# An expert gate that multiplies the centred values and applies 1/std afterwards, in a two-block image kernel on one core

## The chip, the core and the metric

The kernel runs on one core of a Trainium2 chip, as one program. The metric is the device time in microseconds (us) of one execution; lower is better. Seven instruction streams matter here: PE (TensorE, matrix products) with PEld (its weight loads), DVE (VectorE), ACT (ScalarE), POOL (GpSimd), SP (the queue that issues most transfers), and the 16 DMA engines behind them. Every tensor is float32. Each float32 matrix product shows as two records in the trace; a transpose shows as one.

## The reference, cut to what matters

x has 8 images, 32 channels and 24x24 = 576 pixels. Four blocks follow one another, each on normalized values and each added to x: a 3x3 neighbourhood attention, a mixture of 16 experts, a convolution-like block, and a chain of up to 33 data-dependent steps. The change is in the second, which computes, for a layer norm over the 32 channels of each pixel (token):

```
t = (v - mean) / sqrt(var + 1e-5)                 # per token
logits = t @ gate_w.T + gate_b                    # (image, token, expert)
probs  = softmax(logits, over the 576 tokens)
topv, topi = top 8 tokens of each (image, expert)
pooled = sum over the 8 tokens of topv * t[topi]  # (image, expert, channel)
out    = MLP of the expert (weight1, gelu, weight2) on pooled
result[topi] += out * topv
```

The value 1/std belongs to one token of one image; it is the same for all 32 channels and for all 16 experts. The gate bias belongs to one expert, and is the same for all tokens.

## The kernel before, in words

**Layout.** The 8 images are cut into T = 2 halves of TB = 4 images; a half lies as 128 partitions (4 images x 32 channels) by 576 pixels, so a value tile is [128, 2, 576]. The gate's results lie the other way: 128 rows, one per (expert, image) pair, by 576 tokens (`logit`, `rest`, `pick`). A bank of the accumulation memory PS holds 512 values, so a row of 576 takes two products of HS = 288 columns, g = 0 and 1, in two banks.

**Layer norm i** (i = 1 is the one before the experts) goes through three engines. PE centres the values by a product with the matrix `cen` (L621 for i = 0, 2, 3; for i = 1 the products are L729, one for each partial sum of the attention's taps, so that the centred sum grows in PS while the taps come in). ACT squares them from PS (L1067) and copies them to `xc` (L1070). PE sums the squares over channels (`variances`, L631, into 32 rows for each quarter of the pixels, 144 columns). ACT takes the root (L1076), DVE the reciprocal `rstd` (L1238), PE widens it back to 128 rows (`widen`, L644), and DVE multiplies: y = xc * 1/std (L1259). The function `keep_clock` (L615) issues products whose result nobody reads.

**Order.** Each engine runs a list written out by hand, and waits on semaphores. There is no planner. For the expert block PE's list is: the last taps (L729), `variances(1)`, `widen(1)`, the gate product of y (L793, two halves, two products each), ten transposes of y (L800), `preload(0)` (L786, copies centred values into the banks into which results are later added), two products of `keep_clock`, the five transposing products of `pick` with `share` (L811: the selected weights turned to tokens by rows, and divided by the softmax's sum), one `keep_clock`, ten pooling products (L821), and then the expert MLP (L835 to L851) and the scatter (L827). ACT's list is: squares, copy, squares, root, copy of the second half (L1070), load of the table for Exp (L1081), the two halves of `logit` with the bias (L1117), Exp with its sum (L1120), `share` (L1123), three copies of the transposed y to `yT` (L1127), load of the table for Gelu. DVE's list is: `rstd`, y (two halves), the eight largest logits (L1317), their first negated (L1319), the mark of the eight (L1320), the reciprocal of the sum (L1323), `pick` = the eight probabilities, two halves (L1326), the copy of the transposed picks (L1330). POOL meanwhile adds up x after the attention (L559, L563), which ACT waits for at L1129 to L1130. The constants come in three transfers, of which the last, from `hsum` to the table's end (L434), is first needed by the attention's score sums (L711).

Of the kernel before, what the change touches and what calls it, by code (L numbers as in the profile page):

```python
# [7 lines left out]
B, C, HH, WW = 8, 32, 24, 24  # L8
S = HH * WW
P = 128  # L10
# [28 lines left out]
_COLS = [("idn", P), ("cen", P), ("mean", T * 32), ("heads", T * P), ("hsum", T * 32), ("own", B), ("blk", GV), ("blk_end", GV_END),  # L39
         ("ebias", P), ("istep", NB_)]  # L40
OFF, _o = {}, 0
# [6 lines left out]
def constant_table():  # L48
# [32 lines left out]
    e = np.arange(E_)  # L81
    put("ebias", (e[:, None] == p[None, :] // B).astype(np.float32))
    put("istep", 4 * NOPS * np.arange(NB_, dtype=np.float32)[None, :])
    return t
# [7 lines left out]
def metaformer(nc, x, L0_conv_W_trans, L0_ffn_gate_w, L0_ffn_gate_b, L0_ffn_weight1, L0_ffn_weight2,  # L92
# [7 lines left out]
    with ctx:  # L100
# [40 lines left out]
        share = sb("share", [P, P])  # L141
        prob = sb("prob", [P, S])
        pick = sb("pick", [P, S])
# [107 lines left out]
        wc_rep = sem("wc_rep")  # L251
        tail_rdy, bc_ld, bc_set = (sem(n) for n in ("tail_rdy", "bc_ld", "bc_set"))
        row2_done, row2_rdy, row3_rdy = (sem(n) for n in ("row2_done", "row2_rdy", "row3_rdy"))
        waited, wide_first = sem("waited"), sem("wide_first")
# [31 lines left out]

        XB, VB = ((0, 2), (2, 0), (0, 6), (0, 2)), (4, 4, 2, 4)

        def cut(a, t):
# [49 lines left out]
        MAB_BANK = [6, 7, 5, 0, 1]  # L339
        PICK_BANK = (7, 2)  # L340
        PROB_BANK = 2
# [268 lines left out]
        def _(pe):  # L610
# [13 lines left out]
            def variances(i):  # L624

                mean = con("mean").rearrange("p (t m) -> p t m", t=T)
                for t in range(T):
                    for q in range(4):
                        if q % 2 == 0:
                            pe.wait_ge(sq_rdy, 2 * (T * i + t) + q // 2 + 1)  # L630
                        last = nc.tensor.matmul(PS[32 * q:32 * q + 32, VB[i], 0:QS], mean[:, t, :], sq[:, t, q * QS:(q + 1) * QS],  # L631
                                                start=(t == 0), stop=(t == T - 1), skip_group_check=True)
                last.then_inc(var_rdy, 1)
                if i != 2:
                    keep_clock(2, VB[i] + 1)
                    keep_clock(1, VB[i] + 1, 96)

            def widen(i):
# [9 lines left out]
                last.then_inc(rwide_rdy, 1)  # L648
                if i < 2:
                    pe.wait_ge(xc_copied, T * i + 1)  # L650
                    keep_clock(1, XB[i][0] + 1)
# [126 lines left out]
            pe.wait_ge(vadd_rdy, 1)  # L778
            add_tap(14, last=True)
            variances(1)  # L780
            widen(1)


# [4 lines left out]

            for t in range(T):
                pe.wait_ge(xc_copied, 2 * T)  # L790
                pe.wait_ge(y_rdy, T + t + 1)
                for g in range(2):
                    last = nc.tensor.matmul(PS[:, g, 0:HS], gate_bd[:, t, :], cut(y, t)[:, g, :],  # L793
                                            start=(t == 0), stop=(t == T - 1), skip_group_check=True)
                    if t == T - 1:
                        last.then_inc(logit_done, 1)
            for c in range(FULL + 1):
                w = P if c < FULL else TAIL
                for t in range(T):
                    last = nc.tensor.transpose(PS[0:w, 4 + c // 2, ((c % 2) * T + t) * P:((c % 2) * T + t + 1) * P],  # L800
                                               y[:, t, c * P:c * P + w], idn)
                if c % 2 or c == FULL:
                    last.then_inc(yT_done, 1)
            pe.wait_ge(logit_rdy, 2)
            preload(0)
            keep_clock(2, 7)
            pe.wait_ge(share_rdy, 1)
            for c in range(FULL + 1):
                w = P if c < FULL else TAIL
                pe.wait_ge(pick_rdy, 1 if c * P + w <= HS else 2)  # L810
                last = nc.tensor.matmul(PS[0:w, PICK_BANK[c // FULL], (c % FULL) * P:(c % FULL + 1) * P], pick[:, c * P:c * P + w],  # L811
                                        share[:, :], start=True, stop=True, skip_group_check=True)
                if c >= FULL - 1:
                    last.then_inc(pickT_done, 1)
# [51 lines left out]
            def pixels_out(i):  # L866

                if i < T:
                    pe.wait_ge(scat_copied, i + 1)
                pe.wait_ge(y_rdy, 2 * T + T * (i + 1 if i < 2 else NP))  # L870
                for t in range(T):
# [187 lines left out]
        def _(act):  # L1059
            act.dma_start(cst[:, 0:OFF["mean"][0]], consts[:, 0:OFF["mean"][0]]).then_inc(c0_in, 16)  # L1060
            act.dma_start(x_in[:, 1, :], x[TB:B].rearrange("b c h w -> (b c) (h w)")).then_inc(x_ld[2], 16)
            def layernorm(i, eps):
# [13 lines left out]
                nc.scalar.activation(std[:, :], PS[:, VB[i], 0:QS], ACT.Sqrt, bias=eps[:, :]).then_inc(std_rdy, 1)  # L1076
                keep(1)

# [34 lines left out]
            load_table(ACT.Exp)  # L1113
            act.wait_ge(gb_ld, 16)
            for g in range(2):
                act.wait_ge(logit_done, g + 1)
                nc.scalar.activation(logit[:, g * HS:(g + 1) * HS], PS[:, g, 0:HS], ACT.Identity,  # L1117
                                     bias=gb[:, :]).then_inc(logit_rdy, 1)
            act.wait_ge(ntop_rdy, 1)
            nc.scalar.activation(half(0, PROB_BANK), flat2(logit[:, :]), ACT.Exp, bias=ntop[:, :],  # L1120
                                 accum_out=psum_[:, :]).then_inc(prob_rdy, 1)
            act.wait_ge(prec_rdy, 1)
            nc.scalar.activation(share[:, :], idn, ACT.Copy, scale=prec[:, :]).then_inc(share_rdy, 1)  # L1123
            for c in range(0, FULL + 1, 2):
                act.wait_ge(yT_done, c // 2 + 1)
                n, w = (2, P) if c < FULL else (1, TAIL)
                nc.scalar.copy(yT[0:w, c:c + n, :, :].rearrange("k c t p -> k (c t p)"), PS[0:w, 4 + c // 2, 0:n * T * P]).then_inc(yT_rdy, 1)  # L1127
            load_table(ACT.Gelu)
# [99 lines left out]
        def _(dve):  # L1228
# [7 lines left out]
            def layernorm(i, dst, between=None):  # L1236
# [8 lines left out]
                if between:  # L1245
                    between()
                dve.wait_ge(rwide_rdy, i + 1)
                if i == 2:
                    dve.wait_ge(xc_copied, T * i + T)
# [64 lines left out]

            layernorm(1, y)
            dve.wait_ge(logit_rdy, 2)
            nc.vector.max(top8[:, :], logit[:, :]).then_inc(top_rdy, 1)  # L1317
            dve.wait_ge(top_rdy, 1)
            nc.vector.tensor_scalar(ntop[:, :], top8[:, 0:1], -1.0, None, ALU.mult).then_inc(ntop_rdy, 1)  # L1319
            nc.vector.match_replace(rest[:, :], top8[:, :], logit[:, :], -3e38).then_inc(rest_rdy, 1)  # L1320
# [220 lines left out]
```

## Time and profile before

| | |
|---|---|
| median of 3 runs | 117.33 us (117.3 to 118.57) |
| the profiled execution | 117.42 us |
| its span in the trace | 115.4 us |
| PE, DVE, ACT, POOL busy in the span | 102.5, 64.9, 48.3, 65.3 us |
| granted clock of PE | full in all 40 slices |
| expert block, from the last taps' end to the scatter's first product | 50.09 to 69.74 us |

The span is what the trace covers; some 2.0 us of the profiled execution lie around it. "Busy" is the union of an engine's instructions. A busy PE is not a PE at its peak, since the ends of pipelined products are modelled and products that only keep the engine running count too. Times in the trace count from the span's start.

### The profile page before, as it was taken

What the parts mean: (1) busy time and instruction counts of PE and PEld (TensorE: products, weight loads), DVE (VectorE), ACT (ScalarE), POOL (GpSimd) and SP (SyncE); (2) the same over time, 40 slices, a digit from 0 to 9 for tenths busy, and PEclk for the clock granted to TensorE, in tenths of its full rate; (3) what the DMA queues carried; (4) which work ended last, traced back from release to release, by engine and by line L of the source; (5) the groups of instructions that cost most, each with busy time, mean ns of one, the idle gap of its engine ahead of it and who ended that gap; (6) DMA issues with size and microseconds to landing.
All of it is one profiled execution on the core that took longest, in us unless ns stands there. A gap on an engine that the chain in (4) does not pass through costs nothing.

```text
span 115.4 us, 2257 instructions
## 1 busy us (share of the span) xinstructions
PE 102.5 (89%) x825; PEld 66.9 (58%) x825; DVE 64.9 (56%) x150; ACT 48.3 (42%) x103; POOL 65.3 (57%) x68
## 2 busy tenths in 40 slices
PE   6999897986889899998999999898999989986870
PEld 4666654756525347665877675453489766563350
DVE  0019389979589999116263402379716555145891
ACT  4268260209300004055379465622430263685743
POOL 8992079800457988999992000099999950007300
PEclk9999999999999999999999999999999999999999
DMA  3934600000000000000000000000000000100005
GB/s 92 304 27 79 119 0 6 0 6 0 0 0 0 3 0 0 6 0 0 0 0 3 0 6 0 0 3 0 0 6 0 0 0 0 29 6 3 0 6 204
DMA packets 7148, 2.61 MB, mean 23 GB/s; under 512 B 5454, under 2 KB 6624, under 8 KB 7137
## 3 DMA queue, kind: packets, MB, share of 16 engines
q1 hardware_dynamic: 6849, 2.04, 7.7%
q10 hardware_dynamic: 288, 0.43, 1.0%
q8 instruction: 7, 0.11, 0.4%
q14 instruction: 4, 0.03, 0.1%
HBM read 1.87 MB, written 0.59 MB: 21 GB/s over the span
## 4 chain that ended last, share of the span: by engine, by line
PE 58%; DVE 26%; ACT 6%; issue 5%; POOL 2%; DVEq 1%; ACTq 0%; POOLq 0%
DVE prods L1269 7%; PE PS L901 6%; PE PS L744 5%; PE PS L729 5%; PE PS L621 5%; PE PS L615 5%; DVE prods L1307 4%; DVE rstd L1238 4%; PE PS L882 3%; PE PS L827 3%; PE PS L631 3%; PE PS L821 2%; PE PS L644 2%; PE PS L722 2%; PE PS L874 2%
## 5 line engine op out<-in xcount | busy, mean ns | idle before, releaser
L1067 ACT ACTIVATE sq<-PS 128x288 f32<-128x288 f32 x16 | 6.4, 416 | 24.3 <-PE PS L729 18.4
L615 PE MATMUL PS<-sq 128*128 128x288 f32 (+1 forms) x44 | 14.6, 452 | 1.1 <-POOL sq L494 1.1
L1307 DVE TENSOR_TENSOR prods<-PS,vpad 128x432 f32<-128x432 f32 x24 | 12.8, 600 | 1.9 <-PE PS L744 1.6
L535 POOL TENSOR_TENSOR prods<-prods 128x576 f32<-128x576 f32 x8 | 11.7, 1479 | 3.0 <-DVE prods L1307 2.9
L729 PE MATMUL PS<-prods,cst 128*128 128x288 f32 x44 | 12.4, 420 | 0.2 <-POOL prods L535 0.2
L574 POOL TENSOR_TENSOR x<-h,x 128x192 f32<-128x192 f32 x6 | 4.5, 776 | 13.7 <-ACT h L1149 13.6
L729 PEld LDWEIGHTS PS<-prods,cst 128*128 128x128 f32 x44 | 7.8, 189 | 5.5 <-POOL prods L535 1.9
L521 POOL TENSOR_TENSOR prods<-q_sb,kpad 128x576 f32<-128x576 f32 x6 | 7.7, 1320 | 5.6 <-ACT kpad L1095 5.6
L615 PEld LDWEIGHTS PS<-sq 128*128 128x128 f32 x44 | 8.2, 208 | 4.1 <-POOL sq L494 1.1
L1238 DVE RECIPROCAL rstd<-std 128x144 f32<-128x144 f32 x4 | 4.2, 1053 | 11.4 <-ACT std L1076 11.3
L563 POOL TENSOR_TENSOR x<-x,prods 128x576 f32<-128x576 f32 x7 | 9.8, 1405 | 0.5
L1081 ACT ACT_TABLE_LOAD x7 | 9.0, 1283 | 2.2 <-PEq L1524 1.7
L414 POOL TENSOR_TENSOR y<-x,h 128x192 f32<-128x192 f32 x6 | 3.3, 593 | 10.7 <-DVE h L1259 10.7
L1269 DVE TENSOR_TENSOR prods<-PS,kpad 128x576 f32<-128x576 f32 x12 | 8.1, 749 | 2.3 <-ACT kpad L1095 2.3
L744 PE MATMUL PS<-attn,cst 32*128 32x432 f32 x48 | 7.0, 571 | 1.1 <-DVE prods L1307 0.5
L901 PE MATMUL PS<-prods,xT 128*126 128x190 f32 (+3 forms) x46 | 7.4, 310 | 0.0
L528 POOL TENSOR_TENSOR attn<-att,srec 128x432 f32<-128x432 f32 x2 | 2.6, 1302 | 7.7 <-DVE srec L1294 7.7
L685 PE MATMUL PS<-y,qkv_bd 128*128 128x288 f32 x24 | 6.6, 419 | 0.3 <-DVE y L1259 0.3
L1369 DVE TENSOR_TENSOR gram<-PS,cst 126x760 f32<-126x760 f32 (+1 forms) x5 | 4.4, 870 | 4.3 <-PE PS L901 4.3
L711 PE MATMUL PS<-prods,cst 128*32 128x144 f32 x144 | 5.9, 291 | 0.9 <-DVE prods L1269 0.8
L901 PEld LDWEIGHTS PS<-prods,xT 128*126 128x126 f32 (+1 forms) x46 | 6.3, 185 | 0.6 <-issue 0.6
L1172 ACT COPY prods<-PS 64x252 f32<-64x252 f32 (+1 forms) x10 | 3.5, 346 | 7.7 <-PE PS L912 7.6
(166 smaller groups left out, 195.1 us busy)
## 6 DMA issues: line engine op xcount, KB each, us to landing
result<-y SPq DMA_DIRECT2D x2, 288.0 KB, 2.1
prods<-in_x SPq DMA_DIRECT2D x2, 144.0 KB, 2.9
prods<-in_x ACTq DMA_DIRECT2D x1, 288.0 KB, 3.6
cst<-consts SPq DMA_DIRECT2D x1, 261.5 KB, 2.9
ew<-in_L_ffn_weight SPq DMA_DIRECT2D x4, 64.0 KB, 2.3
ew<-in_L_ffn_weight SPq DMA_DIRECT2D x1, 256.0 KB, 2.9
cst<-consts SPq DMA_DIRECT2D x1, 160.0 KB, 2.4
cst<-consts ACTq DMA_DIRECT2D x1, 128.0 KB, 2.9
```

The lines of the kernel that those rows point to most:

```text
L521: nc.gpsimd.tensor_tensor(prods[:, t, n, :].rearrange("p (r c) -> p r c", c=WW), q_sb[:, t, :].rearrange("p (r c) -> p r c", c=WW), kpad[: ...
L535: return nc.gpsimd.tensor_tensor(tap(a), tap(a), tap(b), ALU.add).then_inc(padd_rdy, 1)
L563: last = nc.gpsimd.tensor_tensor(total, total, tap(n), ALU.add)
L615: nc.tensor.matmul(PS[:, bank, 0:width], sq[:, 0, 0:P], sq[:, 0, 0:width], start=True, stop=True)
L685: last = nc.tensor.matmul(PS[:, bank + g, 0:HS], qkv_bd[:, w, :], cut(y, t)[:, g, :], start=True, stop=True)
L729: done = nc.tensor.matmul(PS[:, XB[1][t] + g, 0:HS], con("cen"), src[:, g * HS:(g + 1) * HS], start=first, stop=last, skip_group_check=True)
L744: last = nc.tensor.matmul(PS[:, ring(2 * g + h)[q % 2], 0:TRI * QS], band_of(t, q), attn[32 * q:32 * q + 32, m * TRI:(m + 1) * TRI, :], st ...
L901: last = nc.tensor.matmul(PS[0:w, GRAM_BANK[k] + i // 2, (i % 2) * GV + lo:(i % 2) * GV + hi], xT[:, cols], uT[:, (g0 + i) * GV + lo:(g0 + ...
L1081: nc.scalar.activation(tab[:, :], tab[:, :], f)
L1238: nc.vector.reciprocal(rstd[:, :], std[:, :]).then_inc(rstd_rdy, 1)
L1269: nc.vector.tensor_tensor(prods[:, t, n, :].rearrange("p (g r c) -> p g r c", g=2, c=WW), rows24(half(t, Q_BANK, 4)), kpad[:, t, dy:dy + H ...
L1307: nc.vector.tensor_tensor(prods[:, t, m * TRI:(m + 1) * TRI, q * QS:(q + 1) * QS].rearrange("p n (r c) -> p n r c", c=WW), PS[:, ring(2 * ...
```

## The change

The gate product now reads the centred values `xc` instead of y, and 1/std is applied to its result, in the rows of (expert, image) pairs. A new constant `rows_e` (128 more columns, at the end part of the table) spreads `rstd` to those rows; four products do it in place of eight. DVE's two products that made y are gone; two products of 288 columns make `logit` from the copied gate result and the spread 1/std in PS. `pick` is kept for the scatter, and a scaled `pick_n` = pick * 1/std goes into the pooling, which now reads the transposed `xc`. The bias no longer goes into `logit`; two instructions on 128x1 keep the shift of Exp. The second half of `xc` is copied by DVE in two pieces instead of by ACT. The transposes go to banks 0 and 1, and ACT's copies of them stand ahead of Exp instead of behind `share`. `gate(0)` stands ahead of `variances(1)` in PE's list and `gate(1)` behind it; the three `keep_clock` products of `variances(1)` and the one of `widen(1)` are gone.

```diff
@@ tiles, constant and helpers
-_COLS = [..., ("ebias", P), ("istep", NB_)]
+_COLS = [..., ("ebias", P), ("rows_e", P), ("istep", NB_)]
+    img = (p % 32) // HEADS
+    put("rows_e", ((p[:, None] % HEADS == 0) & (img[:, None] == p[None, :] % B)).astype(np.float32))
+        def by_expert(q):
+            return cst[32 * q:32 * q + 32, OFF["rows_e"][0]:OFF["rows_e"][1]]
+        def wide_e(g):
+            return PS[:, VB[1] + 2 * g:VB[1] + 2 * g + 2, 0:QS]
+        def two(a):
+            return a.rearrange("p (u s) -> p u s", u=2)
-        PICK_BANK = (7, 2)
+        PICK_BANK = (4, 2)
+        GATE_BANK = 2
+        TURN_BANK = (0, 1, 0)
@@ PE: variances, widen
-                if i != 2:
+                if i in (0, 3):
                     keep_clock(2, VB[i] + 1)
                     keep_clock(1, VB[i] + 1, 96)
...
-                if i < 2:
+                if i == 0:
                     pe.wait_ge(xc_copied, T * i + 1)
                     keep_clock(1, XB[i][0] + 1)
@@ PE: the expert block
             add_tap(14, last=True)
+            def gate(t):
+                pe.wait_ge(xc_copied, T + t + 1)
+                for g in range(2):
+                    last = nc.tensor.matmul(PS[:, GATE_BANK + g, 0:HS], gate_bd[:, t, :], cut(xc, t)[:, g, :],
+                                            start=(t == 0), stop=(t == T - 1), skip_group_check=True)
+                    if t == T - 1:
+                        last.then_inc(logit_done, 1)
+            gate(0)
             variances(1)
-            widen(1)
+            gate(1)
+            pe.wait_ge(rstd_rdy, 2)
+            for q in range(4):
+                last = nc.tensor.matmul(PS[:, VB[1] + q, 0:QS], by_expert(q), rstd[32 * q:32 * q + 32, :],
+                                        start=True, stop=True, skip_group_check=True)
+            last.then_inc(rwide_rdy, 1)
-            for t in range(T):
-                pe.wait_ge(xc_copied, 2 * T)
-                pe.wait_ge(y_rdy, T + t + 1)
-                for g in range(2):
-                    last = nc.tensor.matmul(PS[:, g, 0:HS], gate_bd[:, t, :], cut(y, t)[:, g, :],
...
             for c in range(FULL + 1):
                 w = P if c < FULL else TAIL
+                if c == FULL:
+                    pe.wait_ge(yT_rdy, 1)
                 for t in range(T):
-                    last = nc.tensor.transpose(PS[0:w, 4 + c // 2, ...], y[:, t, c * P:c * P + w], idn)
+                    last = nc.tensor.transpose(PS[0:w, TURN_BANK[c // 2], ...], xc[:, t, c * P:c * P + w], idn)
...
-            pe.wait_ge(logit_rdy, 2)
+            pe.wait_ge(yT_rdy, 3)
+            keep_clock(2, 1)
             preload(0)
-            keep_clock(2, 7)
             pe.wait_ge(share_rdy, 1)
             for c in range(FULL + 1):
                 w = P if c < FULL else TAIL
-                pe.wait_ge(pick_rdy, 1 if c * P + w <= HS else 2)
-                last = nc.tensor.matmul(..., pick[:, c * P:c * P + w],
+                pe.wait_ge(pickn_rdy, 1 if c * P + w <= HS else 2)
+                last = nc.tensor.matmul(..., pick_n[:, c * P:c * P + w],
                                         share[:, :], start=True, stop=True, skip_group_check=True)
@@ ACT
-                keep(1)
+                if i != 1:
+                    keep(1)
...
             load_table(ACT.Exp)
-            act.wait_ge(gb_ld, 16)
             for g in range(2):
                 act.wait_ge(logit_done, g + 1)
-                nc.scalar.activation(logit[:, g * HS:(g + 1) * HS], PS[:, g, 0:HS], ACT.Identity, bias=gb[:, :]).then_inc(logit_rdy, 1)
+                nc.scalar.copy(gated[:, g * HS:(g + 1) * HS], PS[:, GATE_BANK + g, 0:HS]).then_inc(gate_copied, 1)
+            for c in range(0, FULL + 1, 2):
+                act.wait_ge(yT_done, c // 2 + 1)
+                ... # the three copies to yT, which stood behind share before
             act.wait_ge(ntop_rdy, 1)
-            nc.scalar.activation(half(0, PROB_BANK), flat2(logit[:, :]), ACT.Exp, bias=ntop[:, :],
+            nc.scalar.activation(half(0, PROB_BANK), flat2(logit[:, :]), ACT.Exp, bias=shift[:, :],
                                  accum_out=psum_[:, :]).then_inc(prob_rdy, 1)
@@ DVE: layernorm, expert block
                 dve.wait_ge(rwide_rdy, i + 1)
+                if i == 1:
+                    for g in range(2):
+                        dve.wait_ge(gate_copied, g + 1)
+                        nc.vector.tensor_tensor(two(logit[:, g * HS:(g + 1) * HS]), two(gated[:, g * HS:(g + 1) * HS]), wide_e(g),
+                                                ALU.mult).then_inc(logit_rdy, 1)
+                    return
...
-            layernorm(1, y)
+            for g in range(2):
+                dve.wait_ge(sq_rdy, 2 * (T + 1) + g + 1)
+                last = nc.vector.tensor_copy(cut(xc, 1)[:, g, :], PS[:, XB[1][1] + g, 0:HS])
+            last.then_inc(xc_copied, 1)
+            layernorm(1, None)
             dve.wait_ge(logit_rdy, 2)
             nc.vector.max(top8[:, :], logit[:, :]).then_inc(top_rdy, 1)
             dve.wait_ge(top_rdy, 1)
-            nc.vector.tensor_scalar(ntop[:, :], top8[:, 0:1], -1.0, None, ALU.mult).then_inc(ntop_rdy, 1)
+            dve.wait_ge(gb_ld, 16)
+            nc.vector.tensor_scalar(ntop[:, :], top8[:, 0:1], gb[:, :], -1.0, ALU.add, ALU.mult).then_inc(max_rdy, 1)
+            dve.wait_ge(max_rdy, 1)
+            nc.vector.tensor_tensor(shift[:, :], ntop[:, :], gb[:, :], ALU.add).then_inc(ntop_rdy, 1)
             nc.vector.match_replace(rest[:, :], top8[:, :], logit[:, :], -3e38).then_inc(rest_rdy, 1)
...
                                                ALU.is_le, ALU.mult).then_inc(pick_rdy, 1)
+                dve.wait_ge(pick_rdy, g + 1)
+                nc.vector.tensor_tensor(two(pick_n[:, cells]), two(pick[:, cells]), wide_e(g), ALU.mult).then_inc(pickn_rdy, 1)
```

## Rows read from the trace of the kernel before

**Rows 1.** Part 1 of the page: busy time of each engine

```profile
PE 102.5 (89%) x825; PEld 66.9 (58%) x825; DVE 64.9 (56%) x150; ACT 48.3 (42%) x103; POOL 65.3 (57%) x68
```

**Rows 2.** Chain of waits, last taps to gate: start us, length us, engine, line, count

```profile
47.88 2.21 PE PS L729 x8
50.09 0.96 PE PS L631 x16
51.08 0.39 ACT std L1076
51.49 1.06 DVE rstd L1238
52.60 0.82 PE PS L644 x16
53.44 0.77 DVE y L1259
54.34 1.71 PE PS L793 x6
```

**Rows 3.** Chain of waits, logits to pooling and on

```profile
56.14 0.94 ACT logit L1117 x2
57.09 0.77 DVE top L1317
57.89 0.17 DVE ntop L1319
58.08 0.88 ACT PS L1120 x2
59.72 1.51 PE PS L811 x10
61.91 2.88 PE PS L821 x20
```

**Rows 4.** Timeline, PE: start us, us, op, shapes, count [idle before]

```profile
7.88 0.77 PE L631 MATMUL PS<-sq,cst 128*32 128x144 f32 x16
```

**Rows 5.** Timeline, ACT and PE: table loads, copies, transposes

```profile
49.64 0.90 ACT L1067 ACTIVATE sq<-PS 128x288 f32<-128x288 f32 x2 [3.89 <-PE PS L729]
51.36 0.63 ACT L1070 COPY xc<-PS 128x576 f32<-128x576 f32 x1
60.88 1.28 ACT L1081 ACT_TABLE_LOAD   x1
62.29 1.14 ACT L1132 COPY prods<-wcT 128x1152 f32<-128x1152 f32 x1
71.76 0.73 ACT L1067 ACTIVATE sq<-PS 128x288 f32<-128x288 f32 x2
56.36 1.25 PE L800 MATMUL PS<-cst,y 128*128 128x128 f32 x10
59.55 1.31 ACT L1127 COPY yT<-PS 128x512 f32<-128x512 f32 x3
```

**Rows 6.** Chain of waits, the last layer norm's widening, four products

```profile
102.48 0.57 PE PS L644 x8
```

**Rows 7.** Groups by form, 44 to 77 us: mean ns of one after the busy time

```profile
L1326 DVE SCALAR_TENSOR_TENSOR pick<-rest,PS 128x288 f32<-128x288 f32 x2 | 0.8, 442 | 0.0
L1330 DVE COPY pickT<-PS 128x512 f32<-128x512 f32 x1 | 0.7, 692 | 1.0 <-PE PS L811 1.0
```

**Rows 8.** Timeline, DVE and POOL: last sum of taps; sum of x; picks

```profile
45.81 0.76 DVE L1312 TENSOR_TENSOR prods<-prods 128x576 f32<-128x576 f32 x1
56.66 4.38 POOL L563 TENSOR_TENSOR x<-x,prods 128x576 f32<-128x576 f32 x3
59.13 0.80 DVE L1326 SCALAR_TENSOR_TENSOR pick<-rest,PS 128x288 f32<-128x288 f32 x2
```

**Rows 9.** PE's waits by line: us in total, times, longest us

```profile
PE PS L722 <- ACT att L1106: 1.5, 1, 1.5
...
PE PS L711 <- DVE prods L1269: 0.8, 4, 0.2
```

More of the change, by code:

```diff
@@ L39 @@
 _COLS = [("idn", P), ("cen", P), ("mean", T * 32), ("heads", T * P), ("hsum", T * 32), ("own", B), ("blk", GV), ("blk_end", GV_END),
-         ("ebias", P), ("istep", NB_)]
+         ("ebias", P), ("rows_e", P), ("istep", NB_)]
 OFF, _o = {}, 0
@@ L141, in metaformer @@
         share = sb("share", [P, P])
-        prob = sb("prob", [P, S])
+        pick_n = sb("pick_n", [P, S])
+        shift = sb("shift", [P, 1])
+        gated = sb("gated", [P, S])
         pick = sb("pick", [P, S])
@@ L252, in metaformer @@
         tail_rdy, bc_ld, bc_set = (sem(n) for n in ("tail_rdy", "bc_ld", "bc_set"))
+        gate_copied, max_rdy, pickn_rdy = (sem(n) for n in ("gate_copied", "max_rdy", "pickn_rdy"))
         row2_done, row2_rdy, row3_rdy = (sem(n) for n in ("row2_done", "row2_rdy", "row3_rdy"))
@@ L787, in preload @@
                                      skip_group_check=True)
-            for t in range(T):
-                pe.wait_ge(xc_copied, 2 * T)
-                pe.wait_ge(y_rdy, T + t + 1)
-                for g in range(2):
-                    last = nc.tensor.matmul(PS[:, g, 0:HS], gate_bd[:, t, :], cut(y, t)[:, g, :],
-                                            start=(t == 0), stop=(t == T - 1), skip_group_check=True)
-                    if t == T - 1:
-                        last.then_inc(logit_done, 1)
             for c in range(FULL + 1):
                 w = P if c < FULL else TAIL
+                if c == FULL:
+                    pe.wait_ge(yT_rdy, 1)
                 for t in range(T):
-                    last = nc.tensor.transpose(PS[0:w, 4 + c // 2, ((c % 2) * T + t) * P:((c % 2) * T + t + 1) * P],
-                                               y[:, t, c * P:c * P + w], idn)
+                    last = nc.tensor.transpose(PS[0:w, TURN_BANK[c // 2], ((c % 2) * T + t) * P:((c % 2) * T + t + 1) * P],
+                                               xc[:, t, c * P:c * P + w], idn)
                 if c % 2 or c == FULL:
                     last.then_inc(yT_done, 1)
-            pe.wait_ge(logit_rdy, 2)
+            pe.wait_ge(yT_rdy, 3)
+            keep_clock(2, 1)
             preload(0)
-            keep_clock(2, 7)
             pe.wait_ge(share_rdy, 1)
@@ L809, in _ @@
                 w = P if c < FULL else TAIL
-                pe.wait_ge(pick_rdy, 1 if c * P + w <= HS else 2)
-                last = nc.tensor.matmul(PS[0:w, PICK_BANK[c // FULL], (c % FULL) * P:(c % FULL + 1) * P], pick[:, c * P:c * P + w],
+                pe.wait_ge(pickn_rdy, 1 if c * P + w <= HS else 2)
+                last = nc.tensor.matmul(PS[0:w, PICK_BANK[c // FULL], (c % FULL) * P:(c % FULL + 1) * P], pick_n[:, c * P:c * P + w],
                                         share[:, :], start=True, stop=True, skip_group_check=True)
@@ L869, in pixels_out @@
                     pe.wait_ge(scat_copied, i + 1)
-                pe.wait_ge(y_rdy, 2 * T + T * (i + 1 if i < 2 else NP))
+                pe.wait_ge(y_rdy, T + T * (i + 1 if i < 2 else NP))
                 for t in range(T):
@@ L1113, in _ @@
             load_table(ACT.Exp)
-            act.wait_ge(gb_ld, 16)
             for g in range(2):
                 act.wait_ge(logit_done, g + 1)
-                nc.scalar.activation(logit[:, g * HS:(g + 1) * HS], PS[:, g, 0:HS], ACT.Identity,
-                                     bias=gb[:, :]).then_inc(logit_rdy, 1)
+                nc.scalar.copy(gated[:, g * HS:(g + 1) * HS], PS[:, GATE_BANK + g, 0:HS]).then_inc(gate_copied, 1)
+            for c in range(0, FULL + 1, 2):
+                act.wait_ge(yT_done, c // 2 + 1)
+                n, w = (2, P) if c < FULL else (1, TAIL)
+                nc.scalar.copy(yT[0:w, c:c + n, :, :].rearrange("k c t p -> k (c t p)"), PS[0:w, TURN_BANK[c // 2], 0:n * T * P]).then_inc(yT_rdy, 1)
             act.wait_ge(ntop_rdy, 1)
-            nc.scalar.activation(half(0, PROB_BANK), flat2(logit[:, :]), ACT.Exp, bias=ntop[:, :],
+            nc.scalar.activation(half(0, PROB_BANK), flat2(logit[:, :]), ACT.Exp, bias=shift[:, :],
                                  accum_out=psum_[:, :]).then_inc(prob_rdy, 1)
@@ L1123, in _ @@
             nc.scalar.activation(share[:, :], idn, ACT.Copy, scale=prec[:, :]).then_inc(share_rdy, 1)
[L1124 to L1127, printed above, removed]
             load_table(ACT.Gelu)
```

## The prediction

> **What bounds the kernel now.** I read the page's busy times first, then the chain of waits, then the timeline and the groups by form of the expert block. PE is busy for 102.5 of 115.4 us [rows 1], but part of that are products that nobody reads, so the share says little; the chain says more. From 47.88 to 61.91 us it passes from engine to engine [rows 2, 3]: taps on PE, squares and variance, root on ACT, reciprocal on DVE, widening on PE, y on DVE, gate product on PE, logits on ACT, maximum on DVE, Exp on ACT, share, then picks turned on PE, then pooling. Each link has nothing beside it that could end later; this is latency. Whatever is taken out of the chain shows in the end, and whatever the engines do beside it does not. The links after pooling are the same instructions in both kernels, so I carry one number: when the pooling's first product starts, 61.91 us in the chain, with its weights ready some 0.2 us earlier (about 61.7).
>
> **Part 1, up to the variance.** gate(0) is put ahead of the variance: two float32 products of 288 columns, four records. Eight such records take 2.21 us [rows 2]; with the last one's length of some 0.4 off, a record costs (2.21 - 0.4)/7 = 0.26, so four cost about 1.0 us on PE. What was there before was not idle-free: the second square half ends at 49.64 + 0.90 = 50.54 [rows 5] and the variance's last quarters waited for it, so its 16 records end at 51.05 [rows 2], while the same 16 with all squares there take 0.77 us [rows 4]. The first record starts near 50.02; after: 50.02 + 1.0 + 0.77 = 51.8. **Cost 0.75 us**; from 0.5 (if the four records stream at 0.2) to 1.0 (if the variance keeps its 0.96).
>
> **Part 2, variance to the maximum.** Before, from 51.05 to 57.09: 6.04 us [rows 2, 3]. After there are two strands, and the later one counts.
> - Root and reciprocal stay, 0.39 and 1.06 with hops of 0.03 to 0.05; the widening has four products instead of eight, and the four of the last layer norm take 0.57 against 0.82 [rows 6, 2]. Spread 1/std is ready at 51.83 + 0.39 + 0.03 + 1.06 + 0.05 + 0.57 = 53.93.
> - ACT: the root ends 52.22. The copy of xc (0.63, [rows 5]) is no longer between it and the table load. In the trace a copy starts 62.29 - 60.88 = 1.41 us after a load starts [rows 5], so the first gate copy starts at 52.24 + 1.41 = 53.65. A pair of 288-column squares takes 0.73 [rows 5] and I price the pair of copies the same: ready at about 54.03 and 54.4. gate(1), two products behind the variance, is done by 51.8 + 1.1 = 52.9, ahead of both.
>
> So ACT is the later strand, by little. DVE then makes the logits: 128x288 against PS cost 0.44 for a similar form [rows 7]; the second starts at 54.43 and ends at 54.87, and the maximum starts at 54.9. **3.1 us instead of 6.04: gain 2.95**. Gone are y (0.77), the gate product (1.71) and the activations (0.94) from the chain, against some 0.9 us of copies and multiplications. Bounds: if the gate copies cost as the old activations, 0.94 for two, the gain is 2.7; if the second copy overlaps more, 3.1.
>
> **Part 3, maximum to Exp.** Before 58.08 - 57.09 = 0.99. The shift is a second 128x1 instruction behind a wait on DVE's own first one; the first of its kind takes 0.17 with its hop [rows 3]. **Cost 0.15** (0.1 to 0.25). The shift also stands ahead of the mark of the eight, which has 0.1 us less room before the sum comes; that is not late. ACT now has the three yT copies, 1.31 us [rows 5], ahead of Exp. Transposes start at about 53.7 at 0.11 us each (1.25 for ten, [rows 5]), so copies can run from 54.4; the fifth chunk waits for the first copy, and PE brings it at about 55.4; the last copy ends near 55.8, and Exp is due at 54.9 + 0.99 + 0.15 = 56.05. Hidden by 0.25 us: the thinnest cover in the change. If it goes, Exp slips by what they are late, a few tenths.
>
> **Part 4, Exp to pooling.** Before 61.7 - 58.08 = 3.6. pick starts 59.13 - 58.08 = 1.05 after Exp [rows 8, 3]. Then each half is pick, wait for it, pick_n, on DVE alone. A pick costs 0.44 [rows 7], two without a wait between 0.80 [rows 8], so an overlapped one adds 0.36 and a hop 0.04: pick_n of half 1 ends 0.44 + 0.04 + 0.36 + 0.44 + 0.04 + 0.44 = 1.76 after the first pick starts. The last three turned chunks need it. From there: two chunks to the end of the fourth, four records of L811, ten of which take 1.51 [rows 3], about 0.7; the copy of four chunks 0.69 [rows 7]; hops 0.15. Sum 1.05 + 1.76 + 0.7 + 0.69 + 0.15 = 4.35. **Cost 0.75 us** (0.5 if pick_n is faster than pick, 0.95 if it doesn't overlap). PE is free for the picks: from the last yT copy at 55.8 its two keep-running and two preload products take 8 x 0.26 = 2.1, to 57.9, and the first pick_n half comes at 58.0.
>
> **Edits at no cost.** DVE's two copies of xc fall where it waited for the root (its reciprocal starts at 51.49, and its last work before ended at 46.6 [rows 2, 8]). The removed keep-running products lay where PE waited for the reciprocal. The constant's 128 x 128 values more are 64 KB in the last of the constants' transfers, which the score sums (L711) read first; these waited only for DVE, never for a transfer [rows 9]. Later ACT waits for POOL's sum of x, which ends at 56.66 + 4.38 = 61.04 [rows 8] whatever the gate does; its 1.4 us of copies then end at 62.5, while pooling would end near 63.4. A gain of over 2.2 us would begin to meet it.
>
> **Sum.** +0.75 - 2.95 + 0.15 + 0.75 = -1.3 us; with a little for hops I have not seen, -1.2. Against the profiled execution's 117.42 that is 116.2; that execution stands 0.09 over the median of 117.33, so I give **116.15 us**, 1.0% faster.
>
> **Rivals.**
> - *A: the front costs more and the thin cover goes.* The variance slips by 1.0, the gate copies cost 0.47 each and the yT copies, 0.25 us ahead of Exp, come late by 0.3; pick_n costs 0.95. -2.7 + 1.0 + 0.45 + 0.95 = -0.3: **117.0**. For it: every one of these is a new instruction whose form the trace does not show. Against: each sits at the end of its bounds at once. Chance 0.2.
> - *B: all the better ends.* -3.1 + 0.5 + 0.1 + 0.5 = -2.0, and the ACT strand a few tenths earlier because the load starts at once: up to -2.5, **114.9 to 115.4**. The bound of POOL's sum then comes into reach. Chance 0.15, of which 0.1 under 115.0.
> - *C: the table load becomes the bound.* It is now on the path, in front of the gate copies. The trace has 1.41 us from the load's start to the next copy's start [rows 5], and I use it. If instead the engine has to be empty for another 1.25 us after the load, the maximum starts at 56.15, and the gain is nothing: **117.4**. The Trainium skill speaks for this one ("ScalarE: Activation LUTs", What ACT_TABLE_LOAD costs): a switch of tables costs 1.28 us of load and 1.38 us of drain, 2.66 in all, by which the change would be worth about 0.05 us. The row disagrees with it here: the load is 1.28 long, and what follows starts 0.13 after its end. Chance 0.05.
> - *D, slower: PE's clock falls.* Full speed (2.4 GHz) is granted throughout; the keep-running products that are removed stood in the wait for the reciprocal. After the change PE waits about 0.5 us before the widening, 0.25 and 0.5 around the last transposes, then works. If the grant falls to 1.2 GHz, every product on the chain takes as long again: turned picks 0.9, pooling 2.88 [rows 3], 3.8 us in all. -1.2 + 3.8 = +2.6: **120.0**, and more if it stays low in the expert products. It decides as soon as the picks and the pooling run below the full clock; less than 3.6 us of loss would end within 2%. Against: PE waited 1.5 us at once in the attention [rows 9], with a full grant in every slice of the page. Chance 0.05. The Trainium skill ("TensorE: Matmul & The Clock Gate", What's actually happening) says that the throttled state is the default and activity releases it, so that taking filler away is a risk; by the rows above the risk is small.
> - *E: not what it says.* The maximum still needs 1/std, which still passes root, reciprocal and spreading; only y, gate product and bias leave. That is in the sum already.
>
> **Numbers.** Forecast 0.55 (115.4 to 116.8), A 0.2, B 0.15, C 0.05, D 0.05. The range 115.1 to 117.6 holds the forecast, A, C and half of B. This kernel's runs differ by about 1%, so 2% (under 115.0, over 119.7) is what can be told from no change. Faster by over 2%: B's lower part, 0.11. Slower by over 2%: D and what I have overlooked, 0.06. Within 2%: 0.83.
>
> **What would show it.** The four gate records between the taps and the variance, and the root starting near 51.8; the first gate copy near 53.65, 1.4 us behind the table load; the maximum near 54.9; Exp near 56.05 with ACT idle a little before it; the second pick_n near 58.9; pooling near 60.4. It is wrong if the granted clock leaves 1.0, if a wait of over 0.3 us stands before Exp on ACT's own list, or if ACT's pooling copies wait for POOL's sum instead of for PE.

## The result, and the profile after

The changed kernel has a median of 118.56 us over 18 runs (115.83 to 119.86), the kernel before, timed again beside it, 118.92 us over 18 runs (117.21 to 120.44). The ratio is 0.9899 with a 95% interval of 0.9857 to 0.9941: 1.0% faster, the ratio that was forecast. The time is not: 118.56 lies outside 115.1 to 117.6. The mean granted clock of PE (1.00 is 2.4 GHz from end to end) goes with the level: in the 18 runs of the changed kernel the five at 0.998 or more took 115.83 to 117.42 us, two at 0.979 took 116.66 and 116.73, and the eleven at 0.971 or less (down to 0.953) 118.38 to 119.86. The ratio leaves disturbed runs out, the medians do not.

The profiled execution of the changed kernel took 115.98 us, its span is 114.1 us; against 117.42 and 115.4 that is 1.44 us. The chain of waits says where (start us, length us, engine, line, count; "..." stands for pieces left out):

```profile
4.39 1.18 PE PS L640 x4
...
47.00 2.21 PE PS L748 x8
49.21 0.97 PE PS L803 x4
50.18 0.67 PE PS L650 x16
50.87 0.38 ACT std L1103
51.27 1.28 ACT L1109
...
52.77 0.29 ACT gated L1144
...
53.15 0.83 DVE logit L1277 x2
54.00 0.77 DVE top L1353
54.80 0.23 DVE ntop L1356
55.05 0.69 DVE shift L1358
55.76 0.88 ACT PS L1150 x2
56.73 0.16 DVE prec L1362
56.90 0.36 DVE pick L1365
57.28 0.45 DVE pick_n L1368
57.73 0.38 DVE pick L1365
58.13 0.47 DVE pick_n L1368
58.64 1.07 PE PS L838 x6
59.72 0.68 PE PS L634 x2
60.40 2.88 PE PS L848 x20
```

L748 answers to L729 of the kernel before, L803 to the gate product L793, L650 to the variance L631, L838 to the turned picks L811, L848 to the pooling L821; L1358 is the new shift. Measured from the first of the last tap products to the first pooling product, the block took 61.91 - 47.88 = 14.03 us before [rows 2, 3] and 60.40 - 47.00 = 13.40 now: **0.63 us**, half of the 1.3 of the prediction's sum. Another 0.88 us is there before the block begins, at 47.00 instead of 47.88, though nothing is changed ahead of it but a longer transfer of constants. It arises in the first centring products. In the kernel before the chain has eight of them:

```profile
4.39 3.32 PE PS L621 x8
```

There the median length of one was 687 ns, against 406 ns in the trace after, where the chain leaves them after four. From the reciprocal that follows (9.12 before, 8.25 after) to the taps the two traces agree, 38.76 and 38.75 us, so the longer transfer costs nothing on that stretch. The profile's page shows a full grant in both traces at the start, so they do not say why the products differ.

By the prediction's parts, the gain is made of:

| | forecast | trace |
|---|---|---|
| 1, taps to the variance's end | +0.75 | 3.85 - 3.17 = +0.68 |
| 2, variance to the maximum | -2.95 | 3.15 - 6.04 = -2.89 |
| 3, maximum to Exp | +0.15 | 1.76 - 0.99 = **+0.77** |
| 4, Exp to pooling | +0.75 | 4.64 - 3.83 = +0.81 |
| sum | -1.30 | -0.63 |

So two things are to be explained: a shift of 128x1 values that takes 0.69 us, and a level of the whole kernel that moves by 3 us from run to run.

### The profile page after: what moved, and what is told of

It reads as the page before. It is cut to its first block, busy times and chain, and to the rows that moved or that the text cites. A ratio compares the mean times of both kernels' runs of the same rounds, so it can differ in the third digit from the quotient of the medians.

```text
span 114.1 us, 2227 instructions
## 1 busy us (share of the span) xinstructions
PE 99.6 (87%) x809; PEld 64.4 (56%) x809; DVE 66.9 (59%) x155; ACT 47.5 (42%) x102; POOL 65.2 (57%) x68
## 4 chain that ended last, share of the span: by engine, by line
PE 56%; DVE 28%; ACT 7%; issue 4%; POOL 2%; DVEq 1%; ACTq 0%; POOLq 0%
DVE prods L1301 7%; PE PS L928 6%; PE PS L763 5%; PE PS L748 5%; PE PS L634 5%; DVE prods L1339 4%; PE PS L909 3%; PE PS L640 3%; PE PS L854 3%; DVE rstd L1264 3%; PE PS L650 3%; PE PS L848 3%; PE PS L741 2%; PE PS L901 2%; PE PS L939 2%
## 5 line engine op out<-in xcount | busy, mean ns | idle before, releaser
L634 PE MATMUL PS<-sq 128*128 128x288 f32 (+1 forms) x36 | 12.5, 467 | 1.6 <-POOL sq L513 1.1
L748 PE MATMUL PS<-prods,cst 128*128 128x288 f32 x44 | 12.4, 420 | 0.2 <-POOL prods L554 0.2
L748 PEld LDWEIGHTS PS<-prods,cst 128*128 128x128 f32 x44 | 7.8, 189 | 5.5 <-POOL prods L554 1.9
L634 PEld LDWEIGHTS PS<-sq 128*128 128x128 f32 x36 | 6.8, 212 | 4.2 <-POOL sq L513 1.1
```

The source lines that it names most:

```text
L634: nc.tensor.matmul(PS[:, bank, 0:width], sq[:, 0, 0:P], sq[:, 0, 0:width], start=True, stop=True)
L748: done = nc.tensor.matmul(PS[:, XB[1][t] + g, 0:HS], con("cen"), src[:, g * HS:(g + 1) * HS], start=first, stop=last, skip_group_check=True)
```

## The experiments

All are edits of one of the two kernels; "the block" is again the time from the first of the last tap products to the first pooling product, read from each kernel's chain of waits.

**a0_after: the changed kernel again.**

> The changed kernel again, on the chip of the next three runs. Between the first of the last tap products and the first pooling product the block took 14.03 us before (47.88 to 61.91) and 13.40 after (47.00 to 60.40): 0.63 shorter, not 1.3. The other 0.88 us of the traces' difference arose before 8 us, where the first centring products took 687 ns each in the trace of before and mostly 406 ns in that of after. Theory 'start by chance': which of the two a run gets has nothing to do with the change; the same code will show either 687 ns or 406 ns again. Theory 'start by the change': the first products are at 406 ns here as well, and at 687 ns whenever the kernel before is traced.

Six runs, median 118.87 us (116.92 to 119.51, all six at a mean clock of 0.978 or less), beside it 119.24 for the kernel before (11 runs, 117.44 to 120.68); ratio 0.9935, interval 0.9752 to 1.0117. The block took 60.08 - 46.68 = 13.40 us, the same to the hundredth. The last taps began at 46.68, so the start was short again; but e1_no_shift, whose edit lies far behind, began them at 47.75, e10_after_filler (the changed code ahead of the tail) at 47.84, and the kernel before's own code, in e9_before_filler, at 46.76. Early and late starts occur with both codes, and over all 14 traces the taps begin anywhere between 46.68 and 47.88: the 0.88 us are no part of the change.

**e1_no_shift: one instruction for the shift.**

```diff
-            dve.wait_ge(gb_ld, 16)
-            nc.vector.tensor_scalar(ntop[:, :], top8[:, 0:1], gb[:, :], -1.0, ALU.add, ALU.mult).then_inc(max_rdy, 1)
-            dve.wait_ge(max_rdy, 1)
-            nc.vector.tensor_tensor(shift[:, :], ntop[:, :], gb[:, :], ALU.add).then_inc(ntop_rdy, 1)
+            nc.vector.tensor_scalar(shift[:, :], top8[:, 0:1], -1.0, None, ALU.mult).then_inc(ntop_rdy, 1)
```

> The two 128x1 instructions that keep the bias in the shift are one again (shift = -largest, as before the change; the bias cancels). Both theories of the 0.68 us shift expect it to go: maximum to Exp 0.99 to 1.0 us instead of 1.76, the block 0.75 shorter than in the changed kernel (12.65), unless the yT copies on ACT, which end at 55.00 there with Exp due then at 55.0, take its place: then 0.5 to 0.7. Against before a ratio of 0.985 to 0.988 if the starts are alike.

Median 117.09 us (6 runs, 115.56 to 118.53, three of them at a mean clock of 0.97 or less), ratio to the kernel before 0.9804 (0.9685 to 0.9923). Maximum to Exp is 55.74 - 54.75 = 0.99 again, the block 12.62 us, 0.78 less. The yT copies cost nothing yet, but their cover is gone:

```profile
54.30 1.45 ACT L1148 COPY yT<-PS 128x512 f32<-128x512 f32 x3 [0.21 <-PE PS L827]
55.55 0.15 DVE L1355 TENSOR_SCALAR shift<-top 128x1 f32<-128x1 f32 x1
55.74 0.75 ACT L1150 ACTIVATE PS<-logit,shift 128x576 f32<-128x576 f32 x1
```

The copies end at 55.75, the shift at 55.70, and Exp follows at once. Whatever makes the maximum earlier from here on meets the copies.

**e3_pool_pause: POOL idle while DVE computes the shift.**

```diff
                 total = xs[1][:, t, :]
+                if t == 1:
+                    pool.wait_ge(ntop_rdy, 1)
                 nc.gpsimd.tensor_tensor(total, x_in[:, t, :], tap(parts[0]), ALU.add).then_inc(x1_part, 1)
```

> POOL waits for the shift before it begins the sum of the second image half, so that it runs nothing while DVE computes the shift; the rest is the changed kernel. Theory 'port' (a DVE instruction with two tensor inputs in SBUF waits until POOL's running instruction ends; in the trace POOL's ended at 55.72 and the shift at 55.73): the shift takes 0.05 to 0.15 us, maximum to Exp 1.1 to 1.2, the block 0.55 to 0.65 shorter. Theory 'form' (a 128x1 product of two tensors behind its own producer costs 0.7): it stays at 0.68. POOL's sum ends about 1 us later, ACT's copies behind it by 62.5 at the latest, before pooling is done: no cost.

The timeline of the changed kernel, DVE and POOL (start us, us, engine, line, operation, tiles, shapes, count):

```profile
54.31 1.41 POOL L578 TENSOR_TENSOR x<-prods 128x576 f32<-128x576 f32 x1
54.80 0.21 DVE L1356 TENSOR_SCALAR ntop<-top,gb 128x1 f32<-128x1 f32 x1
55.05 0.68 DVE L1358 TENSOR_TENSOR shift<-ntop,gb 128x1 f32<-128x1 f32 x1
55.79 4.37 POOL L582 TENSOR_TENSOR x<-x,prods 128x576 f32<-128x576 f32 x3
```

and of e3_pool_pause:

```profile
55.24 0.16 DVE L1360 TENSOR_TENSOR shift<-ntop,gb 128x1 f32<-128x1 f32 x1
55.43 0.75 ACT L1152 ACTIVATE PS<-logit,shift 128x576 f32<-128x576 f32 x1 [0.24 <-DVE shift L1360]
55.48 1.41 POOL L580 TENSOR_TENSOR x<-prods 128x576 f32<-128x576 f32 x1 [0.93 <-DVE shift L1360]
```

The same instruction on the same tiles takes 0.16 us when POOL does nothing, and 0.68 when POOL's addition runs; then it ends 0.01 us behind that addition (55.73 and 55.72). Block 60.07 - 47.20 = 12.87 us, 0.53 less, just short of the 0.55 to 0.65 that were expected. Median of 4 runs 117.69, ratio 0.994 (0.985 to 1.003); every one of them ran at a mean clock of 0.966 to 0.971, so the ratio says less than the trace.

**e2_shift_scalar: the same sum with one tensor input.**

```diff
-            nc.vector.tensor_tensor(shift[:, :], ntop[:, :], gb[:, :], ALU.add).then_inc(ntop_rdy, 1)
+            nc.vector.tensor_scalar(shift[:, :], ntop[:, :], gb[:, :], None, ALU.add).then_inc(ntop_rdy, 1)
```

> The changed kernel with the shift as a tensor-by-scalar instruction: the same sum of the same two 128x1 tiles, but the bias is read as the per-row scalar operand, so there is one tensor input instead of two. Theory 'port': 0.15 to 0.2 us as the instruction ahead of it (0.21), though POOL's instruction runs beside it; maximum to Exp 1.2 to 1.25 instead of 1.77. Theory 'any DVE instruction on 128x1 behind its producer and beside POOL': 0.6 to 0.7.

The timeline:

```profile
54.31 1.40 POOL L578 TENSOR_TENSOR x<-prods 128x576 f32<-128x576 f32 x1
54.79 0.21 DVE L1356 TENSOR_SCALAR ntop<-top,gb 128x1 f32<-128x1 f32 x1
55.04 0.21 DVE L1358 TENSOR_SCALAR shift<-ntop,gb 128x1 f32<-128x1 f32 x1
55.29 0.74 ACT L1150 ACTIVATE PS<-logit,shift 128x576 f32<-128x576 f32 x1 [0.30 <-DVE shift L1358]
```

POOL's addition stands beside it as before, and the shift takes 0.21. So it is neither the size nor the dependence: it is the form with two tensor inputs in SBUF. The larger tensor_tensors of the block, with one input in PS, are not held up by POOL either: the two of `logit` take 0.82 together and each `pick_n` 0.45, beside a running addition of POOL. Block 12.93 us. Only one run was made, 117.55 us.

**e4_gates_late: both gates behind the variance.**

```diff
-            gate(0)
             variances(1)
+            gate(0)
             gate(1)
```

> gate(0) stands behind variances(1) instead of ahead of it. By the prediction's part 1 the four gate records in front cost 0.68 us of the variance's end: it now ends 3.15 to 3.2 us after the first of the last tap products instead of 3.85. The gates then end 2.1 us later, near the end of the reciprocal: ACT's first gate copy is due 1.8 us behind the root's start and may wait for PE by 0.1 to 0.3, and the spreading products start 0.2 to 0.4 late behind the gates. Theory 'gate ahead is pure cost': the maximum comes 0.5 to 0.65 earlier. Theory 'it only moves the wait': 0.3 or less.

```profile
53.61 0.76 DVE L1353 MAX8 top<-logit 128x8 f32<-128x576 f32 x1
54.28 1.40 POOL L578 TENSOR_TENSOR x<-prods 128x576 f32<-128x576 f32 x1
54.41 0.21 DVE L1356 TENSOR_SCALAR ntop<-top,gb 128x1 f32<-128x1 f32 x1
54.66 1.04 DVE L1358 TENSOR_TENSOR shift<-ntop,gb 128x1 f32<-128x1 f32 x1
55.73 0.75 ACT L1150 ACTIVATE PS<-logit,shift 128x576 f32<-128x576 f32 x1 [0.96 <-DVE shift L1358]
```

The variance's end came 0.7 us earlier (the root starts 50.15 - 46.95 = 3.20 behind the taps, 3.87 in the changed kernel), the maximum 0.33 (6.66 and 7.00), since the gates now delay the spreading. Exp came no earlier: the shift is 1.04 us long and ends with the same POOL addition. The block is 13.42. What is won upstream of a wait for another engine's running instruction is lost in it. Median 119.24 (6 runs, all at a mean clock of 0.952 to 0.971), ratio 1.0053 (0.9965 to 1.014).

**e5_both: e1 and e4 together.**

> No shift instruction, and both gates behind the variance. With the gates late alone the maximum came 0.33 us earlier (6.66 instead of 6.99 after the first of the last tap products) and Exp came no earlier (8.78 against 8.77), because the shift then took 1.04 us, up to the end of the same POOL instruction. Theory 'port': without the shift both gains count, Exp starts 6.66 + 0.99 = 7.65 after the taps (7.99 without the shift alone), the pooling 12.1 to 12.2 (12.46). Theory 'the yT copies' (they end 7.8 to 7.85 after the taps there and stand ahead of Exp): Exp starts at 7.85, the pooling at 12.3.

Median 117.82 us over 13 runs (115.06 to 118.33), ratio 0.9824 (0.9751 to 0.9897). Exp starts 54.85 - 47.13 = 7.72 behind the taps, between the two expectations: the yT copies, which end last there, cost some 0.06. The block is 12.36 us. The 0.33 of the late gates, nothing in e4, count here with 0.26.

**e7_mark_first: part 4 done otherwise** (the edit condensed; the fifth turned chunk goes to bank 5, and PE waits for pick before it writes bank 3).

```diff
+            scaled_mark(0)          # (rest <= -3e38) * wide_e(0), while Exp runs
             dve.wait_ge(prob_rdy, 1)
             nc.vector.reciprocal(prec[:, :], psum_[:, :]).then_inc(prec_rdy, 1)
             for g in range(2):
-                pick[g] = (rest <= -3e38) * prob;  pick_n[g] = pick[g] * wide_e(g)
+                if g == 1: scaled_mark(1)
+                pick_n[g] = mark[g] * prob
+            for g in range(2): pick[g] = (rest <= -3e38) * prob
```

> e5_both with part 4 done otherwise: the mark of the eight times 1/std is made first (half 0 during Exp), pick_n is then one product with Exp's result, and pick follows it off the path. If part 4 (0.8 us) is the price of four dependent DVE instructions behind Exp, three of which now remain and one stands ahead of the sum's reciprocal: Exp to the second pick_n's end 2.4 to 2.5 us instead of 2.82, pooling 0.3 to 0.4 earlier than in e5_both. Rival: DVE is not the bound there but PE, which finishes preload and filler first: then below 0.1.

Exp to the second pick_n's end: 57.48 + 0.45 - 55.48 = 2.45 us instead of 2.82, block 12.01, 0.35 under e5_both. So the dependent DVE instructions behind Exp bounded this part. Of its 0.81 us, 0.35 are taken back. In the new chain PE's unread and preload products run from 55.63 to 57.83, right up to the turned picks, so by this chain a faster DVE alone would gain little more. Its 4 runs have a median of 118.39, three of them at a mean clock of 0.952 to 0.967.

**e6_filler_back: an unread product in the wait for the reciprocal.**

```diff
             gate(1)
+            keep_clock(1, VB[1] + 1)
```

> The changed kernel with one unread product put back behind gate(1), in the wait for the reciprocal that the prediction calls free. It runs from about 51.9 to 52.5 us where the spreading products are due at 52.39: theory 'the removed filler was free': at most 0.1 to 0.2 later for the spreading, nothing at the maximum, since ACT's copies are the later strand by 0.13. Theory 'filler on the edge': 0.2 to 0.4 later.

One run, 118.63 us at a mean clock of 0.971. The spreading products start 52.71 - 47.32 = 5.39 behind the taps as in the changed kernel (5.39), the maximum at 7.00 (7.00). The block is 13.41 us. The one product that was put back, of four removed, is free, and so is its absence: in none of the 14 traces did the clock fall in the block.

**e8_tail_filler: e5_both with one more unread product near 102 us.** The level of the whole kernel's time is set in another place. In the trace of a0_after (stretch, its length, busy us and count of PE, PEld, DVE, ACT, POOL; then PE's granted clock):

```profile
102.00:104.00 2.00, 1.02 (x8) 0.59 (x11) 1.29 (x2) 1.35 (x3) 1.29 (x3) 1.00 0.04 12
104.00:106.00 2.00, 1.90 (x20) 0.76 (x12) 1.13 (x4) 1.11 (x3) 2.00 (x4) 1.00 0.00 0
106.00:108.00 2.00, 1.92 (x16) 0.89 (x16) 1.73 (x3) 1.48 (x2) 0.05 (x1) 0.61 0.00 0
108.00:110.00 2.00, 2.00 (x28) 1.10 (x28) 1.10 (x4) 0.75 (x2) 0.00 (x0) 0.54 0.00 0
```

The clock falls from 2.4 to 1.2 GHz (1.00 to 0.5) in the last steps, behind a stretch in which PE waits for h, the input of the last block's products. The eight traces with such a fall take 54.8 to 57.3 us from the first pooling product to the end of the span, the six whose clock holds until PE's last product 53.5 to 54.2. The wait alone does not decide: the first trace of the same code has the same 0.98 us of it and no fall.

```diff
-            keep_clock(1, 1)
+            keep_clock(2, 1)
             pe.wait_ge(xc_copied, 4 * T)
```

> e5_both with one more product that nobody reads, in PE's wait for h at about 102 us, in the last block. In four of five traces of the kernels after the change PE's granted clock fell to 0.5 for some microseconds from 104 to 106 us on, behind a stretch of 2 us with 0.95 to 1.0 us of PE work, and those runs are 1 to 3 us longer; the kernel before shows the same two levels of time. Theory 'the gap': the fall is less frequent or gone, mean clock 0.99 to 1.0 in most runs, median near 115.5. Theory 'chance or the steps behind': the clocks are spread as in e5_both, medians within 0.5 of each other.

```profile
102.00:104.00 2.00, 1.41 (x18) 0.92 (x20) 0.59 (x2) 0.63 (x3) 2.00 (x5) 1.00 0.01 4
104.00:106.00 2.00, 1.77 (x16) 0.71 (x13) 1.70 (x5) 1.62 (x3) 1.10 (x3) 1.00 0.00 0
106.00:108.00 2.00, 1.64 (x32) 1.15 (x32) 1.92 (x5) 1.48 (x2) 0.00 (x0) 1.00 0.00 0
```

Median 115.48 us (6 runs, 115.12 to 117.73) against 117.82 of e5_both on the same chip: 2.3 us in the median from one product whose result nobody reads, while the runs of both at full clock are alike (lowest 115.12 and 115.06). Ratio to the kernel before 0.9833 (0.9765 to 0.9902). Four of the six had a mean clock of 1.0; of e5_both's 13, three.

**e9_before_filler and e10_after_filler: the same product in the kernel before and in the changed one.**

> The kernel before with the one added product in the last block's wait, nothing else. If the low clock of the tail is a property of that gap and not of the change, the kernel before gains by it too: mean clock 1.0 in most runs, median 117.2 to 117.7 instead of 119.2 to 119.7, lowest time unchanged at 117.2.

> The changed kernel with the same product. With the tail steady in both, the difference to e9_before_filler is the change itself: the expert block is 0.62 us shorter in the traces, and the start's 687 or 406 ns products fall by chance on either. Theory 'block only': median 0.4 to 0.9 under e9_before_filler, lowest time about 115.8 or 116.6 as the start falls. Theory 'the change helps elsewhere too': 1.2 and more under it.

| 12 runs each, one chip | median us | lowest to highest | mean clock under 0.99 | block us |
|---|---|---|---|---|
| before, with it | 117.34 | 116.58 to 118.67 | 4 | 14.02 |
| changed, with it | 116.86 | 116.04 to 117.39 | 0 | 13.41 |
| before, without | 118.29 (23 runs) | 116.86 to 185.24 | 12 | 14.03 (first trace) |

With the tail steadier the change is worth 117.34 - 116.86 = 0.48 us, or 0.54 by the lowest times; the block alone explains 0.61. Theory "block only" fits, the 1.2 us and more of the other do not. In the kernel before the product's effect on the clock is less sure than in e8: 4 of 12 runs under 0.99 against 12 of 23 may be chance. The ratios to the kernel before were 0.997 (0.993 to 1.001) and 0.9937 (0.9898 to 0.9976).

**e11_mark_filler: everything together.**

> e7_mark_first with the same product: shift gone, gates late, the mark of the eight scaled first. The pooling starts 11.85 us after the taps (11.83 in e7_mark_first, 12.20 in e5_both, 13.24 in the changed kernel by the timeline), so 0.35 under e8_tail_filler: lowest 114.7 to 114.8, median 115.0 to 115.4; ratio to the kernel before 0.965 to 0.97 by medians, 0.978 to 0.98 by runs at full clock.

Median 115.19 us (6 runs, 114.94 to 115.84) against 118.29 of the kernel before on that chip; ratio 0.9803 (0.9748 to 0.9859). The block is 12.02 us. It is the fastest of these kernels, against the kernel before by 2.0% in the ratio and 2.6% in the medians; the interval leaves open whether it is over 2%. The median is as expected, the lowest time and both ratios are just short of it.

## Why the prediction was wrong, and where it was right

**The time missed through its level.** The step that failed is the last of the working, "This kernel's runs differ by about 1%", with the range built on it, and behind it rival D's "with a full grant in every slice of the page". Three runs, and one profile at full clock, stood for the kernel; the 18 runs beside the result spread over 2.8%. Over 50 further runs of the kernel before (11, 17 and 22 on three chips; one outlier of 185 us left out), 32 had a mean clock under 0.99 and took 117.6 to 120.7 us; the other 18 took 116.9 to 118.3. At full clock the forecast was good: the five such runs of the changed kernel have a median of 116.0. The fall is not D's: in every trace of the changed kernel and its variants that shows one, it comes 35 us or more behind the block. For the kernel before, only mean clocks say that it falls, since both traces of its code ran at full clock to PE's last product. Of the 39 runs of a0, e1, e3, e4, e5 and e7, 32 were under 0.99; of the 36 with the added product (e8, e9, e10, e11), 5. Chips and kernels are mixed in these two counts; on one chip it is 13 of 17 (e5, e7) against 1 of 6 (e8). Whether the change itself makes the fall more frequent (19 of 24 runs of the changed kernel, 32 of 50 of the one before), and what decides from run to run, stays open. The Trainium skill ("TensorE: Matmul & The Clock Gate", What's actually happening) has the throttled state as the default that activity releases; e8 agrees in that with one more product, of no other use, the clock held at 1.00 in four runs of six.

**The ratio was right by luck.** The block's gain was forecast at 1.3 and is 0.63. The step that failed is part 3, the shift at 0.15 us (bounds 0.1 to 0.25): it is 0.77, and explains 0.62 of the 0.67 us that are missing. I took its price from the only 128x1 instruction of the chain, which has one tensor input, listed POOL's sum only as something ACT would wait for later, and held that "whatever the engines do beside it does not" show in the end. The new instruction is a tensor_tensor with both inputs in SBUF, and e3 and e2 show what that means: it waits for POOL's running instruction. The Trainium skill ("SBUF — State Buffer", Who interferes with whom) states it, that a VectorE instruction with two SBUF inputs and a GpSimd instruction that reads SBUF exclude one another for a whole instruction; the traces agree for a VectorE instruction that comes second, with 0.68 and 1.04 us beside POOL and 0.16 without; the other order no run here shows. What fills the gap up to the forecast is no part of the change: in the pair of profiles it is the start, whose 0.88 us fall by chance and made 1.44 of 0.63. The measured ratio is 0.990, where block and e9/e10 stand for 0.995 to 0.996, which its interval (0.9857 to 0.9941) does not hold. That this too comes from the starts and clocks that the 18 runs drew is likely but not shown; the repetition, 0.9935 with an interval of 0.9752 to 1.0117, holds both.

**Parts 1, 2 and 4 held** to 0.07, 0.06 and 0.06 us. gate(0) costs 0.68 in front of the variance (e4 takes it off). ACT was the later strand, by little: the timeline after has

```profile
51.27 1.28 ACT L1109 ACT_TABLE_LOAD   x1
52.39 0.53 PE L813 MATMUL PS<-rstd,cst 32*128 32x144 f32 x8 [0.42 <-DVE rstd L1264]
52.67 0.66 ACT L1144 COPY gated<-PS 128x288 f32<-128x288 f32 x2
53.15 0.82 DVE L1277 TENSOR_TENSOR logit<-gated,PS 128x288 f32<-128x288 f32 x2 [0.81 <-ACT gated L1144]
```

The spread 1/std is ready at 52.92 and the first gate copy at 53.06. That copy starts 1.40 us behind the table load's start, so rival C is refuted. The Trainium skill ("ScalarE: Activation LUTs", What ACT_TABLE_LOAD costs) has 2.66 us for a switch; the trace does not agree, and the measurement decides. The yT copies stayed hidden, behind a shift that was itself late; they end level with it in e1_no_shift and cost 0.06 in e5_both, where Exp comes earlier. Part 4 was mainly the DVE chain (e7). Rivals A and B did not occur: A's mechanisms kept to the forecast, and what cost 0.6 us was none of them. Of the edits called free, e6 tests the removed unread products and the stretch ahead of the taps the transfer; DVE's two copies of xc were not tested apart, but part 1 leaves no cost for them. POOL's sum, named as a limit for ACT, was a limit for DVE. One slip stands in the numbers of the forecast: B, with 0.1 of its 0.15 put under 115.0, cannot lie by half in a range that starts at 115.1.

## What to carry to other kernels

Price a new instruction by its form, not its size: a tiny VectorE instruction with two SBUF inputs beside a busy GpSimd costs up to the rest of GpSimd's instruction, and swallows what is gained ahead of it; a scalar-operand form (0.21 us in e2) or an input in PS (`logit`, `pick_n`) avoids it. Before you change the middle of a kernel, read the granted clock of several runs and not of one: here one unread product in a wait of the last block was worth 2.3 us in the median of one kernel (e8), more than the whole change. And compare traces from a landmark just ahead of the change, since what lies before it may differ by chance.

## What the runs showed of the hardware

- The first eight centring products took 2.10 to 3.53 us from trace to trace, in both codes (median length of one between 406 and 687 ns), with 1.00 as the granted clock in that stretch. What decides between the two stays open.
- A DVE tensor_tensor of 128x1 with both inputs in SBUF took 0.16, 0.68 or 1.04 us, by how long POOL's addition still ran; it ended 0.01 to 0.02 us behind that addition.
- In the changed kernel and its variants the first ACT copy behind a table load started 1.40 us after the load's start; the load itself took 1.28.
- Mean clocks of whole runs cluster, at 1.00, 0.985, 0.97, 0.965 and 0.953. In e4 and e7 a second fall (0.57 and 0.50) stands at 96 to 98 us, and nothing was tried against that one.
- A mean clock a little under 1.00 need not cost anything: in the traces of e9 and e11, both at 0.993, the grant is 1.00 up to PE's last product (before 111 us) and falls only behind it.
